# Flamingo layer: q and k as two float32r parts, two heads in the row halves of the array, and a new order of products in a step

## What is computed

```
q = heads(layernorm(x) @ Wq.T + bq); k = heads(ctx @ Wk.T + bk); v = heads(ctx @ Wv.T + bv)   # 16 heads of 16
attn = softmax(q @ k.T / sqrt(16)); x = x + tanh(g_xattn) * (attn @ v -> merged @ Wo.T + bo)
x = x + tanh(g_ffn) * (top-2-of-8 experts + shared expert)(layernorm(x))
```

## Time and profile before

| | before |
|---|---|
| time, median of 3 runs | 459.9 us (459.63 to 461.47) |
| profiled execution, span from first to last instruction | 466.8 us |
| PE busy in it | 453.6 us, 97% |
| DVE busy | 331.8 us, 71% |
| ACT busy | 252.6 us, 54% |
| POOL busy | 154.4 us, 33% |
| mean granted TensorE clock | 0.993 |

### The profile page before, as it was taken

The page is one execution under the profiler, slowest core; times in us unless marked ns, Lnnn a source line. Parts: engine busy times, 40 slices in busy tenths (PEclk is TensorE's granted clock), DMA queues, the critical chain, the costliest instruction groups (busy, mean ns, idle before and its releaser), DMA issues.

```text
span 466.8 us, 8100 instructions
## 1 busy us (share of the span) xinstructions
PE 453.6 (97%) x2310; PEld 215.8 (46%) x2310; DVE 331.8 (71%) x841; ACT 252.6 (54%) x540; POOL 154.4 (33%) x209
## 2 busy tenths in 40 slices
PE   8999999999999999999999989889999999999997
PEld 8664432222222222222465634565555555555745
DVE  1988898888888888888578766354565656532674
ACT  2664477777777777777565111023666766631110
POOL 5493488111212121212132766600323332332000
PEclk9999999999999999999999999979999999999999
DMA  8669762335353535353548522311322222312921
GB/s 261 223 181 251 157 204 58 86 83 97 90 98 94 98 94 97 95 92 102 167 135 264 211 91 81 110 48 46 93 84 88 85 88 83 90 49 60 377 101 47
DMA packets 54140, 56.71 MB, mean 121 GB/s; under 512 B 13456, under 2 KB 44560, under 8 KB 54096
## 3 DMA queue, kind: packets, MB, share of 16 engines
q1 hardware_dynamic: 47504, 43.82, 34.1%
q0 software_dynamic: 4960, 10.53, 7.4%
q10 hardware_dynamic: 1632, 1.84, 1.2%
HBM read 36.35 MB, written 17.72 MB: 116 GB/s over the span
## 4 chain that ended last, share of the span: by engine, by line
PE 90%; DVE 4%; issue 2%; DMA 1%; SPq 1%; another core or an unknown queue 1%; POOL 1%; ACT 1%; DVEq 0%; POOLq 0%
PE PS L1395 13%; PE PS L1305 13%; PE PS L1523 12%; PE PS L1567 11%; PE PS L1677 9%; PE PS L1580 6%; PE PS L1696 5%; PE PS L1357 4%; PE PS L1672 3%; PE PS L1442 3%; PE PS L1691 2%; PE PS L1651 2%; DVE nmax L842 2%; PE PS L1335 2%; PE PS L1659 2%
## 5 line engine op out<-in xcount | busy, mean ns | idle before, releaser
L842 DVE TENSOR_REDUCE nmax<-PS 128x1 f32<-128x512 f32 x256 | 159.4, 683 | 21.4 <-PE PS L1305 21.4
L730 ACT ACTIVATE R<-PS 128x512 f32<-128x512 f32 x256 | 134.1, 601 | 42.0 <-PE PS L1523 41.7
L1305 PE MATMUL PS<-R 96*128 96x512 bf16 x256 | 96.1, 382 | 1.2 <-DMA R<-k_parts 1.0
L1523 PE MATMUL PS<-R 98*128 98x512 bf16 x256 | 86.2, 380 | 0.3 <-DVE R L860 0.3
L1395 PE MATMUL PS<-R 128*32 128x512 f32 x512 | 68.2, 604 | 0.0
L621 POOL DMA_INDIRECT token_y<-R,dest x34 | 32.6, 960 | 93.4 <-DVE R L1184 92.0
L1305 PEld LDWEIGHTS PS<-R 96*128 96x128 bf16 x256 | 24.8, 97 | 69.7 <-DVE nmax L842 51.1
L1677 PE MATMUL PS<-R 128*128 x100 | 47.3, 595 | 0.2 <-ACT R L798 0.2
L745 ACT ACTIVATE R<-PS 128x512 f32<-128x512 f32 x16 | 9.6, 597 | 68.7 <-PE PS L1567 52.1
L600 POOL DMA_DIRECT2D CH<-R x56 | 27.4, 496 | 54.4 <-ACT R L718 54.4
L1523 PEld LDWEIGHTS PS<-R 98*128 98x128 bf16 x256 | 24.8, 97 | 38.6 <-ACT R L730 22.6
(11 more groups left out here) (177 smaller groups left out, 598.4 us busy)
## 6 DMA issues: line engine op xcount, KB each, us to landing
R<-q_parts SPq DMA_DIRECT2D x96, 64.0 KB, 3.1
R<-k_parts SPq DMA_DIRECT2D x96, 64.0 KB, 3.1
R<-in_fc_w_dram SPq DMA_DIRECT2D x16, 256.0 KB
R<-token_y SPq DMA_DIRECT2D x4, 1024.0 KB, 9.0
R<-slot_x SPq DMA_DIRECT2D x25, 129.0 KB
k_parts<-R SPq DMA_DIRECT2D x8, 384.0 KB, 3.3
q_parts<-R SPq DMA_DIRECT2D x8, 384.0 KB, 3.5
fc<-in_fc_w_dram SPq DMA_DIRECT2D x16, 128.0 KB
```

What stands on the lines that cost most here:

```text
L730: nc.scalar.activation(PT[:, kt, j, :], PS[:, (G * (TB * i + kt) + j) % 3, :], ACT.Exp).then_inc(exp_done, 1)
L842: nc.vector.tensor_reduce(nmax[:, i % 2, j * TB + qt:j * TB + qt + 1], PS[:, smax_bank(n), :], AX.X, ALU.max, negate=True).then_inc(max_re ...
L1305: mm(PS[:, smax_bank(n), :], QS[g][0:KS, j, qt * P:(qt + 1) * P], KST[g][0:KS, j, :], start=True, stop=True).then_inc(smax_done, 1)
L1523: mm(PS[:, n % 3, :], KST[g][0:KM, j, kt * P:(kt + 1) * P], QS[g][0:KM, j, :], start=True, stop=True).then_inc(st_done, 1)
```

## The change

- q and k are cut into two parts instead of three: the first rounded to float32r by ACT, the second the float32 difference, written by DVE. `second_part` and `third_part` go. Three products of parts remain: 48 rows a head.
- Two heads stand in one tile: head r of a pair in rows 64 r to 64 r + 47, the two maximum rows below them. A score or maxima product uses rows of one half of the array, on float32r operands (4 bytes, 512 moving columns, as before). The 12 transfers of a group stay 12 of 64 KB; the stored chunk grows from 384 to 512 KB.
- The order of maxima tiles alternates between the two halves, and the loop's are reduced two banks at a time (`two_max`); 28 instead of 24 are made in the setup, up to four behind a chunk.
- The maxima are cut on DVE before the transpose (`split_max`), 32 columns are transposed, into a bank of the scores' rotation, and one ACT copy (`max_rows`) replaces `m_first` and `m_second`. `values` moves from bank 6 to bank 3, the loop's maxima to banks 4 to 7.
- In a step the products stand in a new order; the copy of the outputs and of the maxima move on ACT's list.

```diff
-    TERMS = 6
-    Q_PART = [0, 1, 2, 0, 1, 0]
-    K_PART = [0, 0, 0, 1, 1, 2]
+    TERMS = 3
+    Q_PART = [0, 1, 0]
+    K_PART = [0, 0, 1]
+    UNIT = 2 * TERMS
+    HALF = P // 2
...
+        with nc.sbuf_tensor("QK", [P, 8192], F32R) as QK:
+            pass
...
-        EARLY = 6 * G
+        EARLY = 7 * G
-        EARLY_J = ((0, 0, 0, 0), (0, 0, 0, 0), (2, 2, 2, 2), (2, 2, 2, 2))
+        EARLY_J = ((0, 0, 0, 0), (0, 0, 0, 0), (2, 2, 2, 2), (2, 2, 4, 4))
+        MT_AT = 2 * G + 2
+        def score_turn(i, kt, j):
+            return (G * TB + 1) * i + G * kt + j + (i + 1 < GROUPS and G * kt + j >= MT_AT)
...
-            return (6, 4, 5)[n % 3] if n < EARLY else 3 + n % 3
+            return (6, 4, 5)[n % 3] if n < EARLY else 4 + (n - EARLY) % 4
...
-            def second_part(b, j):
-                act.wait_ge(rest_ready, 4 * b + j + 1)
-                nc.scalar.copy(QP[:, j, 1, :], REST[:, j, :]).then_inc(q2_ready, 1)
...
+            def two_max(n):
+                i, _, at = max_tile(n)
+                for r in range(2):
+                    dve.wait_ge(smax_done[r], n // 2 + 1)
+                nc.vector.tensor_reduce(nmax[:, i % 2, at:G * TB:G * TB // 2], PS[:, smax_bank(n):smax_bank(n) + 2, :], AX.X,
+                                        ALU.max, negate=True).then_inc(max_ready, 1)
+            def split_max(i):
+                dve.wait_ge(max_ready, maxima(G * TB * (i + 1)))
+                if i >= 2:
+                    dve.wait_ge(mt_done, i - 1)
+                nc.vector.tensor_copy(nmax_parts[:, i % 2, 0, :].bitcast(F32R), nmax[:, i % 2, :]).then_inc(high_max, 1)
+                dve.wait_ge(high_max, i + 1)
+                nc.vector.tensor_tensor(nmax_parts[:, i % 2, 1, :], nmax[:, i % 2, :], nmax_parts[:, i % 2, 0, :],
+                                        ALU.subtract).then_inc(split_ready, 1)
...
-                    mm(PS[:, n % 3, :], KST[g][0:KM, j, kt * P:(kt + 1) * P], QS[g][0:KM, j, :],
-                       start=True, stop=True).then_inc(st_done, 1)
+                    turn = score_turn(i, kt, j)
+                    turn_free(turn)
+                    h, r = divmod(j, 2)
+                    at = slice(HALF * r, HALF * r + KM)
+                    mm(PS[:, turn % 3, :], KST[g][at, h, kt * P:(kt + 1) * P], QS[g][at, h, :],
+                       start=True, stop=True).then_inc(st_done[r], 1)
...
+                    mx[0]()
+                    mx[1]()
                     scores(kt, 0)
                     scores(kt, 1)
-                    mx[0]()
-                    scores(kt, 2)
-                    mx[1]()
                     if kt == 2 and i + 1 < GROUPS:
                         max_transpose(i + 1)
+                    scores(kt, 2)
+                    mx[2]()
+                    mx[3]()
+                    scores(kt, 3)
                     if kt:
                         values(i, kt - 1)
...
-                    mx[2]()
-                    scores(kt, 3)
-                    mx[3]()
```

More of the change, by code:

```diff
@@ L10 @@
 F32 = mybir.dt.float32
-BF16 = mybir.dt.bfloat16
+F32R = mybir.dt.float32r
 U32 = mybir.dt.uint32
@@ L281, in bank @@
         def bank(kind, b, part=0):
-            return 3 + USERS.index((kind, b, part)) % 3
+            return 4 + USERS.index((kind, b, part)) % 3
         def gu_bank(n, k):
@@ L288, in gu_bank @@
                 return k
-            return (2, 6)[k] if n < IC + 2 else 2 + k
+            return 2 + k
         def down_bank(b, t):
@@ L675, in m_first @@
                     act.wait_ge(m_in[i % 2], 32 * (i // 2))
-                nc.scalar.copy(mparts[:, i % 2, 0, :], PS[0:G * TB, 7, 0:P]).then_inc(m1_ready, 1)
+                nc.scalar.copy(mparts[:, i % 2, :], PS[0:2 * G * TB, max_turn(i) % 3 if i else 7, 0:P]).then_inc(m_ready, 1)
             def load_context(b):
@@ L733, in _ @@
                             h2t_first(n // 2 - 1)
-                        if j == 2 and kt == 0 and i:
+                        if j == 0 and kt == 1 and i:
                             out_copy(i - 1)
-                        if j == 1 and kt == 2 and i + 1 < GROUPS:
-                            m_first(i + 1)
+                        if G * kt + j + 1 == MT_AT and i + 1 < GROUPS:
+                            max_rows(i + 1)
             out_copy(GROUPS - 1)
@@ L898, in _ @@
             early_max(EARLY - sum(map(sum, EARLY_V + EARLY_J)))
-            def head_max(s):
-                for qt in range(TB):
-                    one_max(TB * s + qt)
             def scale_of(i):
@@ L953, in h2t_second @@
                 dve.wait_ge(h2_t, 2 * b + 2)
-                dve.wait_ge(st_done, G * TB * (GROUPS - 1 + b // 2))
+                for r in range(2):
+                    dve.wait_ge(st_done[r], G // 2 * TB * (GROUPS - 1 + b // 2))
                 nc.vector.tensor_copy(H2T[:, 1, b * S:(b + 1) * S], PS[:, bank("h2_t", b, 1), :]).then_inc(h2t_ready[1], 1)
@@ L1298, in scores_for_max, with turn_free @@
                 if n == 14:
[L1299 removed]
+                    pe.wait_ge(low_ready, 4 * (B - 1))
                 if n == 15:
                     pe.wait_ge(va_ready, 7)
[L1302 to L1303 removed]
+                if n == EARLY + 3:
+                    pe.wait_ge(m_ready, 1)
                 wait(pe, max_ready, max_user(n))
[L1305 to L1315 removed]
+                mm(PS[:, smax_bank(n), :], QS[g][at, h, qt * P:(qt + 1) * P], KST[g][at, h, :],
+                   start=True, stop=True).then_inc(smax_done[n % 2], 1)
+            def turn_free(turn):
+                i, m = divmod(turn - 3, G * TB + 1)
+                if turn < 3:
+                    return
+                if i + 1 < GROUPS and m == MT_AT:
+                    pe.wait_ge(m_ready, i + 2)
+                else:
+                    pe.wait_ge(exp_done, G * TB * i + m - (i + 1 < GROUPS and m > MT_AT) + 1)
+            def max_transpose(i):
+                pe.wait_ge(split_ready, i + 1)
+                if i:
+                    turn_free(max_turn(i))
+                nc.tensor.transpose(PS[0:2 * G * TB, max_turn(i) % 3 if i else 7, 0:P],
+                                    nmax_parts[:, i % 2, :, :].rearrange("p a n -> p (a n)"), ident[:, :]).then_inc(mt_done, 1)
             early = iter(range(EARLY))
```

217 lines of the change are left out of this document (95 added, 122 removed).

## The result

The kernel after takes 481.2 us (median of 4 runs, 480.8 to 485.0) against 460.7 for the one before: a ratio of 1.047, 95% interval 1.041 to 1.052. (Some runs of a kernel are slower at a lower granted clock; ratios leave out those over 1.5% above its fastest, medians and ranges hold all of them.) The predicted time was 471.6, its range 456 to 488. The profiled execution's span went from 466.8 to 479.1 us, where 478.7 was predicted. So the span was hit within 0.4 us while the timed difference was 20.5 us and not 11.7; that disagreement is the first thing to explain.

What follows compares the result with a forecast made beforehand. PE's amount of work was taken to bound the kernel before, a chain over the exponential the one after. Four terms (+2.5, +3.8, +1.9, +3.7) summed to +11.9 of span, 459.9 + 11.7 = 471.6 us; range 456 to 488.

Steps and rivals of the forecast that it cites:

- E: Part of a weight load on PE that nothing covers: 0.105 us for float32r, 0.01 as the other end, twice per step.
- Cheap loads: Rival: float32r weight loads as cheap as bf16's (0.01 us), giving 458.4 us, no change; chance 0.22.
- term 1: Regular loop, 57 steps from first to 58th value products: 166.9 against 164.4 us, +2.5.
- The clock rival: PE idling about 0.5 us a step lowers the clock, doubling the chain's streaming: +76, about 547 us; chance 0.02.
- Term 2: Last steps: each goes from 1.98 to 2.78 us through the wait for the exponential and shape changes, together +3.8.
- Terms 3 and 4: Setup to the third chunk's end of the last batch, +1.9; from there to the first value products, +3.7.
- Serial halves: Rival: two row halves of a pair run one after the other, +14.5, so 486 us; chance 0.09.
- slow float32r: Rival: 512 float32r columns stream at 0.43 us instead of 0.22, +40, about 511 us; chance 0.05.
- a free order: Rival: the order does not bind, the step going at PE's 2.2 or DVE's 2.4 us: 440 us; chance 0.04.

Runs made afterwards that it cites:

- experiment 1: Kernel after with the first maxima pair moved behind the first two scores of a step: 465.6 us, ratio 1.012 to the kernel before.
- experiment 5: Three separate edits of the kernel after: 24 early maxima, 478.5 us; unused products filling setup waits (the filled one), 476.9 to 489.2 us; second maxima pair issued twice, 479.3 us.
- experiment 4: Kernel after with the fourth score put behind the value products in the last six steps: 481.3 us, ratio 1.045 to the kernel before.
- the second kernel of experiment 6: Kernel after with scores first, 24 early maxima placed evenly, late fourth score in last steps, first maxima split one piece earlier: 462.8 us, ratio 1.009 to before.
- The order-only kernel: Kernel before (bf16, six products, full array) with only the new step order and the outputs' copy moved: 465.3 us, ratio 1.011 to the kernel before.
- experiment 6: Kernel after with scores first, 24 early maxima and late fourth score in last steps: 465.8 us; second kernel 462.8; that with the second maxima pair doubled 466.0.
- experiment 7: The 462.8 us kernel with four score banks, single-bank maxima reductions from three banks, values ahead of second pair and fourth score, old copy place: median 494.2 us, ratio 1.054.

## Why the prediction was right, and where it was not

- **Direction and mechanism: right, and shown.** The step is the chain values, pair, first score, exponential, fourth score. Its links agree with the rows within 0.03 each; taking the pair out of it gives 0.23 a step (experiment 1), doubling a pair beside it gives 0 in a plain step (experiment 5).
- **E, the uncovered load: slightly under-sized.** 0.11 to 0.12 for 0.105. Cheap loads are refuted by the 0.19 us records and the 0.50 against 0.39 us matmuls. With the way from the load to the values (0.43 for 0.405) and 0.14 instead of 0.06 for the copy, a group came to 12.0 for 11.72: 13 groups make +3.6 on term 1.
- **Term 1 failed in size.** +2.5 predicted, +12.7 measured: 4.0 from the links above and 6.2 from the clock.
- **The clock rival: right in kind, wrong in chance and size.** It had 0.02 and a price of 76 us for a whole loop. What happened in the profiled execution is a fall for 17 us at the start of the loop, worth 6.2. Of the other runs only mean clocks are recorded: by an estimate (twice the missing share, times the span) 0.979 and 0.982 are 17 to 20 us at the lower level, and 0.968, the run of 485.0 us, is some 30. The prediction looked for gaps in the steady step, and asked whether the clock would fall for good; the larger gaps were at the end of the setup, where PE is busy 12.16 of 15 us in 55:70, though gaps there alone don't explain the fall (below). A fall that ends by itself was not among the cases, though the earlier trace rows hold one.
- **Term 2: right.** Predicted +3.8, measured +3.9. A last step grew by 0.84 (3.70 to 4.54) for the predicted 0.80, and without the wait it shrinks by 0.53 (experiment 4).
- **Terms 3 and 4: right within 0.7.** To the end of the third chunk +1.9 predicted and +2.2 measured, from there to the first values +3.7 and +4.1; the scatter of the start, up to 1.5, is larger than these differences. The waits on DVE behind the chunks and at the loop's second tile are those named; the one at 68.21 was not.
- **The base was not checked.** The sum was made on a profiled span that held a stall of about 10 us. The text set it beside the median of the runs as "1.5% high" and scaled the difference down with it, instead of asking where in the profile those 7 us lay; the earlier trace rows showed the place. A base 10 us too high and a loop term 10 us too low cancel, which is why the span agrees within 0.4 us. That agreement is luck. The forecast time, 459.9 + 11.7, does not rest on the base but on the difference, and it is 9.6 under the measured 481.2.
- **Serial halves, slow float32r, a free order:** refuted by the pair's 0.50 us, the 0.39 us of a 512-column float32r matmul in the place of 0.59, and the wait on ACT.

What stays open: what makes the clock fall. PE's busy time before it does not decide. Experiment 1 has nearly the same setup as after (busy 12.22 of 15 us in 55:70, 12.16 in after) and kept the full clock in its profiled execution; in the second kernel of experiment 6 it fell after 14.38 of 15. The order-only kernel (13.95 of 15.4) and before (14.46 of 15) kept it there, with mean clocks of 1.00 and of 0.995 to 1.00 in their other runs. Every kernel with float32r halves has a mean clock under 1.00 in all of its runs, but for one run of experiment 1. So a rival stands that no run separates from PE's gaps: that the form of the products (48 or 50 rows of one half, float32r) has a part in it. A cure was not found, and filling the setup's waits gave no readable answer. The 2.1 us between the parts' sum and the timed difference are open as well.

## What to carry to other kernels

Where PSUM banks rotate through another engine, write the loop as a chain from a score to the user of its bank three turns on, and put the largest block of independent work between them: here moving one pair by two places was worth 0.23 a step, 13 us of the loop (15.6 by the times, part of it the clock's), and moving one transpose behind the value products about 4 (0.27 in each of 15 groups), while halving a product's rows took nothing off a step that a chain sets. A turn given to a rare helper (the transpose) costs a wait once a group unless a large block covers it.

Before summing on a profiled span that stands above the runs, find where the excess lies; if it can't be found in one place, price both bases. And price a fall of the clock that ends by itself, not only one for good: the falls seen here last 3.4 to 27 us and cost microseconds each, most of them at the start of the loop, but in experiments 6 and 7 also in the middle of it.

## What the runs showed of the hardware

- A float32r load of 128 columns is recorded at 0.18 to 0.19 us, as float32's, and leaves 0.11 us uncovered behind a wait, while the float32r matmul of 512 columns takes 0.39 us with slots of 0.23, as bf16's 0.38 and 0.22. The Trainium skill ("TensorE: Matmul & The Clock Gate", "Weight-path perf modes") has fast weight load off for FP32 inputs; this trace agrees if float32r is counted as FP32 for the load.
- The change between a step's other products and the value products in column quarters costs about 0.1 us of PE each way, for full-height bf16 as for float32r in row halves.
- A two-bank reduction on DVE (1024 elements a partition) is recorded at 1217 ns, a single one at 683 to 685. In a step two double ones take 2.36 us in a row and four single ones 2.49 (experiment 7), so 0.13 is gained, less than the records suggest.
- The granted clock fell to the lower level for 17 us at the start of after's loop (PE busy 12.16 of the 15 us up to 70) and came back inside the loop by itself. It also fell after 14.38 of 15 (experiment 6) and did not after 12.22 of 15 (experiment 1). Mean clocks of one and the same kernel ranged from 0.965 to 0.996 (experiment 5, the filled one).
- PE can stand still for 0.8 to 1.5 us several times with no releaser in the profile (300 to 305 us of before); after the second of three such gaps the clock was at the lower level for 6.8 us.
